# Squares in three fp32r passes: splitting the first layer's products and beginning VectorE's chain among ScalarE's first banks

## The reference

```python
B, M, D = (1024, 39, 16)
S1, S2 = (128, 128)
def _cin_layer(x0, xk, W, b):
    out = jnp.einsum('bhd,bmd,shm->bsd', xk, x0, W) + b[None, :, None]
    return jax.nn.relu(out)
e = jnp.stack([tbl_0[ids[:, 0]], ..., tbl_38[ids[:, 38]]], axis=1)
x1 = _cin_layer(e, e, W1, b1)
x2 = _cin_layer(e, x1, W2, b2)
z = jnp.concatenate([x1.sum(axis=-1), x2.sum(axis=-1)], axis=-1)
h = jnp.concatenate([z, dense_ctx], axis=1)
h = jnp.maximum(h @ W_top1 + b_top1, 0.0)
h = jnp.maximum(h @ W_top2 + b_top2, 0.0)
y = h @ W_top3
```

## Time and profile before

| | |
|---|---|
| median of three executions | 1232.25 us |
| profiled execution: time, span | 1228.31 us, 1226.4 us |
| TensorE, matmul | 1172.4 us busy, 96% |
| VectorE | 1005.4 us, 82% |
| ScalarE | 672.1 us, 55% |
| GpSimd | 864.8 us, 71% |

### The profile page before, as it was taken

The page is one execution under the profiler, slowest core; times in us unless marked ns, Lnnn a source line. Parts: engine busy times, 40 slices in busy tenths (PEclk is TensorE's granted clock), DMA queues, the critical chain, the costliest instruction groups (busy, mean ns, idle before and its releaser), DMA issues.

```text
span 1226.4 us, 17749 instructions
## 1 busy us (share of the span) xinstructions
PE 1172.4 (96%) x4784; PEld 879.4 (72%) x4784; DVE 1005.4 (82%) x3692; ACT 672.1 (55%) x2188; POOL 864.8 (71%) x836
## 2 busy tenths in 40 slices
PE   3899999999999999999999999999999999999996
PEld 2577777777777777777776667777777777777775
DVE  4298898888899888888896678888888888887695
ACT  2656666665565656556564465555655565545430
POOL 7888878888888788788776757888886454444350
PEclk9899999999999999999999999999999999999997
DMA  5000000000000000000000000000000000000000
GB/s 177 5 4 4 4 4 3 4 4 5 3 4 3 4 3 3 4 4 3 4 4 3 3 3 3 4 3 4 3 4 2 1 1 1 1 1 1 1 1 1
DMA packets 12801, 9.08 MB, mean 7 GB/s; under 512 B 6190, under 2 KB 11822, under 8 KB 12573
## 3 DMA queue, kind: packets, MB, share of 16 engines
q0 software_dynamic: 10240, 2.64, 2.6%
q1 hardware_dynamic: 2461, 5.31, 1.3%
HBM read 7.92 MB, written 0.00 MB: 6 GB/s over the span
## 4 chain that ended last, share of the span: by engine, by line
PE 72%; DVE 18%; ACT 5%; issue 2%; POOL 2%; DMA 0%; SPq 0%; ACTq 0%
PE ps L724 17%; PE ps L726 17%; PE ps L725 17%; DVE acc L634 15%; PE ps L702 13%; PE ps L690 3%; PE ps L755 3%; ACT e L464 2%; ACT fy L425 2%; POOL looked L339 2%; DVE x1l L595 1%; PE ps L678 1%; DVE e_hl L580 1%; PE ps L697 0%; DVE e_hl L583 0%
## 5 line engine op out<-in xcount | busy, mean ns | idle before, releaser
L634 DVE SCALAR_TENSOR_TENSOR acc<-ps,e,acc 128x128 f32<-128x128 f32 x3200 | 854.4, 343 | 155.7 <-PE ps L726 152.4
L724 PE MATMUL ps<-w2h,x1h 128*128 128x512 f32 (+1 forms) x1280 | 582.4, 455 | 24.9 <-ACT fy L425 13.8
L348 POOL TENSOR_TENSOR fy<-fy 128x512 f32<-128x512 f32 (+1 forms) x256 | 403.0, 1574 | 214.3 <-ACT fy L425 193.5
L425 ACT ACTIVATE fy<-ps,e 128x128 f32<-128x128 f32 x1536 | 418.1, 387 | 198.8 <-PE ps L726 198.3
L726 PE MATMUL ps<-w2h,x1l 128*128 128x512 f32 (+1 forms) x1280 | 495.4, 387 | 0.0
L725 PE MATMUL ps<-w2l,x1h 128*128 128x512 f32 (+1 forms) x1280 | 494.3, 386 | 0.0
L339 POOL DMA_INDIRECT looked<-in_table,rows x320 | 310.9, 972 | 79.1 <-issue 55.0
L724 PEld LDWEIGHTS ps<-w2h,x1h 128*128 128x128 f32 x1280 | 241.5, 189 | 134.1 <-DVE acc L634 50.9
L725 PEld LDWEIGHTS ps<-w2l,x1h 128*128 128x128 f32 x1280 | 241.6, 189 | 82.6 <-issue 44.7
L726 PEld LDWEIGHTS ps<-w2h,x1l 128*128 128x128 f32 x1280 | 240.7, 188 | 48.4
L444 ACT ACTIVATE z<-ps 128x512 f32<-128x512 f32 x192 | 117.9, 614 | 224.8 <-PE ps L690 219.5
(11 more groups left out here) (64 smaller groups left out, 385.5 us busy)
## 6 DMA issues: line engine op xcount, KB each, us to landing
looked<-in_table,rows POOLq DMA_INDIRECT x320, 2.3
w_st<-in_w SPq DMA_DIRECT2D x1, 1728.0 KB, 10.2
wt_sb<-in_wt SPq DMA_DIRECT2D x2, 512.0 KB
w_st<-in_w SPq DMA_DIRECT2D x1, 768.0 KB, 6.3
w_sb<-in_w1a SPq DMA_DIRECT2D x1, 448.0 KB, 3.2
w1b_sb<-in_w1b SPq DMA_DIRECT2D x1, 448.0 KB, 3.8
sel_st<-in_sel SPq DMA_DIRECT2D x1, 234.0 KB
ids_sb<-in_ids SPq DMA_DIRECT2D x1, 150.0 KB, 4.9
```

The costliest lines, as they stand in the source:

```text
L348: nc.gpsimd.tensor_tensor(out, a, b, ALU.add).then_inc(s_fsum, 1)
L425: nc.scalar.activation(fy[:, p % 2, sub, m - MD, :], ps[:, 2 * (nth % RING) + sub, k * S:(k + 1) * S], ACT.Copy, scale=emb(p, sub, m)).the ...
L634: nc.vector.scalar_tensor_tensor(acc[:, sub, :] if m < MD - 1 else y, y, emb(p, sub, m), acc[:, sub, :] if m else fsum[:, p % 2, sub, :], ...
L724: nc.tensor.matmul(y, x1h[:, t % 2, at], w2h[:, cols], start=True, stop=False)
```

## The change

It has three parts.

1. From tile 2 on, chunks 0, 2, 3 and 5 of the squares are split. ScalarE writes a rounded square zh, and then squares once more in place in PSUM; VectorE subtracts (zl = square - zh); TensorE takes three fp32r matmuls in place of one fp32 matmul. The next use of PSUM bank 7 waits for zl. The first layer's weights are split once at the start (w1h by ScalarE, w1l by VectorE).
2. The first banks are ordered anew: A0, D0, A1, D1, A2 of pair 0, and then the rest of pair 0 with five A banks between. In pairs 0 and 1 VectorE's chain starts with a multiplication alone, and fsum is added just before the last field. ScalarE makes the half w2h for its fields. Products of the low part of the first bank wait for x1l, the others for x1h alone.
3. TensorE runs 28 matmuls without use before the first transpose. Steps of the perceptron at slots 14 and 16 of a tile move to 8 and 14. hid1, hid2 and y_sb are laid over w2_st.

The diff, cut to its core:

```diff
+SPLIT, SPLIT_FROM = (0, 2, 3, 5), 2
+LATE = 2
+WARM = 28
 def bank_order():
-    slots = [[("A", 0, a) for a in range(A_BANKS)] + [("A", 1, a) for a in range(EARLY)]]
-    for p in range(PAIRS):
+    slots = [[("A", 0, 0), ("D", 0, 0), ("A", 0, 1), ("D", 0, 1), ("A", 0, 2)]]
+    first = (("D", 0, 2), ("D", 0, 3), ("A", 1, 0), ("D", 0, 4), ("D", 0, 5), ("A", 1, 1), ("D", 0, 6), ("A", 1, 2), ("A", 2, 0))
+    slots += [[bank] for bank in first] + [[]]
+    for p in range(1, PAIRS):
...
+def split_after(p, j):
+    slots = [s for s, kind in enumerate(ORDER) if kind == "D"] + [SLOTS]
+    return [at for s in range(slots[j], slots[j + 1]) for at in layer1_steps(p, s) if is_split(*at)]
...
-    for c, s in enumerate((0, 4, 14, 16)):
+    for c, s in enumerate((0, 4, 8, 14)):
...
-    MLP_AT[TILE_SLOTS * (tile + 1) + 14] = (g, 3, 0)
+    MLP_AT[TILE_SLOTS * (tile + 1) + 8] = (g, 3, 0)
... (ScalarE)
+                    if is_split(t, v):
+                        nc.scalar.activation(zh[:, k % 2, :], src, ACT.Square).then_inc(s_z1, 1)
+                        nc.scalar.activation(src, src, ACT.Square).then_inc(s_sq, 1)
+                    else:
+                        nc.scalar.activation(z1[:, k % 2, :], src, ACT.Square).then_inc(s_z1, 1)
...
+                nc.scalar.activation(w2h[:, MD * S:], w2_st[:, MD * S:], ACT.Copy, scale=0.5).then_inc(s_w2h, 1)
+                nc.scalar.activation(w1h[:], w1_sb[:, 0:C1, :], ACT.Copy).then_inc(s_w1h, 1)
... (VectorE)
+                def square_low(t, v):
+                    k = C1 * t + v
+                    dve.wait_ge(s_sq, splits(t, v))
+                    if k >= 2:
+                        dve.wait_ge(s_mm1, k - 1)
+                    nc.vector.tensor_tensor(zl[:, k % 2, :], ps[:, BK_T, :], zh[:, k % 2, :], ALU.subtract).then_inc(s_zl, 1)
...
+                            if m == MD - 1 and p < LATE:
+                                dve.wait_ge(s_fsum, ADDS_PER_PAIR * (p + 1))
+                                dve.wait_ge(s_stt, n)
+                                for sub in range(2):
+                                    nc.vector.tensor_tensor(acc[:, sub, :], acc[:, sub, :], fsum[:, p % 2, sub, :],
+                                                            ALU.add).then_inc(s_late, 1)
...
+                        for at in split_after(p, j):
+                            square_low(*at)
... (TensorE)
-                            pe.wait_ge(s_z1, C1 * at[0] + at[1] + 1)
+                            if is_split(*at):
+                                pe.wait_ge(s_zl, splits(*at))
+                            else:
+                                pe.wait_ge(s_z1, C1 * at[0] + at[1] + 1)
...
+                    if is_split(t, v):
+                        nc.tensor.matmul(ps[:, BK_ACC1, :], w1h[:, v, :], zh[:, k % 2, :], start=False, stop=False)
+                        nc.tensor.matmul(ps[:, BK_ACC1, :], w1l[:, v, :], zh[:, k % 2, :], start=False, stop=False)
+                        pe.wait_ge(s_zl, splits(t, v))
+                        mm = nc.tensor.matmul(ps[:, BK_ACC1, :], w1h[:, v, :], zl[:, k % 2, :], start=False, stop=(v == C1 - 1))
...
+                for _ in range(WARM):
+                    nc.tensor.matmul(ps[:, C1 - 1, :], sel_r[:, 0, :], sel_r[:, 0:N // K1, :].rearrange("p c k -> p (c k)"),
+                                     start=True, stop=True)
```

More of the change, by code:

```diff
@@ L120, in layer1_steps, with is_split, splits @@
     return [(t, k // 2)] if t < TILES and k % 2 == 0 and k // 2 <= C1 and slot >= 11 else []
+def is_split(t, v):
+    return t >= SPLIT_FROM and v in SPLIT
+def splits(t, v):
+    return sum(is_split(u, w) for u in range(t + 1) for w in range(C1) if (u, w) <= (t, v))
+def split_after(p, j):
+    slots = [s for s, kind in enumerate(ORDER) if kind == "D"] + [SLOTS]
+    return [at for s in range(slots[j], slots[j + 1]) for at in layer1_steps(p, s) if is_split(*at)]
 def put_by_dve(f):
@@ L209, in cin_tower @@
         wz = sb("wz", [P, S], F32R)
+        w1h = sb("w1h", [K1, C1, S], F32R)
+        w1l = sb("w1l", [K1, C1, S], F32R)
         fold_sb = sb("fold_sb", [K1, C1, M])
@@ L215, in cin_tower @@
         z1 = sb("z1", [P, 2, N])
+        zh = sb("zh", [P, 2, N], F32R)
+        zl = sb("zl", [P, 2, N], F32R)
         x1 = sb("x1", [S, 2, N])
@@ L265, in cin_tower @@
         s_wz = sem("s_wz")
+        s_w1h = sem("s_w1h")
+        s_w1l = sem("s_w1l")
         s_z1 = sem("s_z1")
+        s_sq = sem("s_sq")
+        s_zl = sem("s_zl")
+        s_late = sem("s_late")
         s_mm1 = sem("s_mm1")
@@ L328, in _ @@
                 sp.wait_ge(s_tail, 7)
-                sp.dma_start(out, y_sb[:]).then_inc(s_out, 16)
+                sp.dma_start(out, y_sb).then_inc(s_out, 16)
                 sp.wait_ge(s_out, 16)
@@ L513, in _ @@
                 high_part(1)
[L514 to L517, removed]
+                for n, (kind, p, j) in enumerate(BANK_SLOTS[0]):
+                    if kind == "A":
+                        scaled_fields(p, j)
+                    if n == 0:
+                        products_high(1)
+                    if n == 3:
                         turned(1)
@@ L613, in _ @@
                 low_part(0)
-                dve.wait_ge(s_w2a, 16)
-                split_w2(slice(MD * S, M * S))
+                dve.wait_ge(s_w2h, 1)
+                w2_low(slice(MD * S, M * S))
                 dve.wait_ge(s_w2d, 16)
-                split_w2(slice(0, MD * S))
+                nc.vector.tensor_scalar(w2h[:, 0:MD * S], w2_st[:, 0:MD * S], 0.5, None, ALU.mult).then_inc(s_w2h, 1)
+                dve.wait_ge(s_w2h, 2)
+                w2_low(slice(0, MD * S))
+                dve.wait_ge(s_w1h, 1)
+                nc.vector.tensor_tensor(w1l[:], w1_sb[:, 0:C1, :], w1h[:], ALU.subtract).then_inc(s_w1l, 1)
                 first_layer_low(0)
@@ L633, in _ @@
                                 y = ps[:, 2 * (nth % RING) + sub, k * S:(k + 1) * S]
+                                if m == 0 and p < LATE:
+                                    nc.vector.tensor_scalar(acc[:, sub, :], y, emb(p, sub, m), None, ALU.mult).then_inc(s_stt, 1)
+                                    n += 1
+                                    continue
                                 nc.vector.scalar_tensor_tensor(
```

43 lines of the change are left out of this document (26 added, 17 removed).

## The result

| | before | after |
|---|---|---|
| median (us) | 1232.4 | 1261.1 (1259.54 to 1263.33) |
| ratio | | 1.0234 [1.0216, 1.0251] |
| profiled execution, span | 1228.31, 1226.4 | 1260.78, 1258.9 |

The forecast was 1250, range 1224 to 1257. The direction came out, and so did the waits for zl that were to make the tiles slower; the sum did not: the time lies 4 us above the range. A second measurement on another chip gave 1254.92 beside 1226.96, ratio 1.0225 [1.0208, 1.0242]. The traced execution of before is 4.1 us shorter than its median, that of the changed kernel is at it, so the spans lie 32.5 us apart where the medians lie 28.7 apart.

What follows compares the result with a forecast made beforehand. TensorE (96% busy) was taken as bound, with stretches where VectorE sets the end. Steady state -21.6+5.4+17.5+11.1+4.7 = +17.1 us, start +1.3, on the profiled 1228.3: 1246.7; median 3.9 higher, 1250.6, called 1250, range 1224 to 1257.

Steps and rivals of the forecast that it cites:

- The gain on TensorE: Split products on TensorE: three passes take 0.68 us in place of 0.86, 120 times, 21.6 us less.
- Chunk 5 gains nothing: Chunk 5's product, behind D2 of the even pair: TensorE waits afterwards for what it saves, 5.4 us of the gain go.
- The wait for zl of chunk 0: Odd pair: chunk 1's expansion comes 4.88 us after J, D0's start on VectorE, at the earliest; 17.5 us lost together.
- The wait for zl of chunk 3: Behind D5: chunk 4's expansion waits until 4.88 us after D4's start, 0.37 us 30 times, 11.1 us lost.
- The zl of chunks 2 and 5: They lie in VectorE's idle time and cost nothing; without that cover each would cost up to 0.7 us.
- Steady state: Sum over the tiles of passes, chunk 5, both zl waits and restarts: +17.1 us.
- restart: First TensorE matmul after each wait takes 0.33 us instead of 0.23; booked as 59 x 0.08 = 4.7 us.
- The start: Up to chunk 1's expansion in tile 0's odd pair: 77.7 us against 76.37 before, +1.3 us.
- w1l and w2h: Weight splits at the start: new w1l on VectorE, w2h's smaller part leaving it, about balancing in cost to look-ups.
- the waits don't bind: Rival: VectorE's zl arrives in time and TensorE keeps its pace; about 1212 us, or 1207; chance 0.14.
- Slower by ScalarE: Rival: two squares delay ScalarE's scalings 0.5 us, fsum comes later, VectorE's D0 waits; 1250, up to 1260 us; chance 0.09.
- VectorE's share: Sign in the profile after: VectorE is busy 87 to 88% of the time.

Runs made afterwards that it cites:

- e7: e5 with chunk 5 unsplit, its product fp32 again: 1213.60 us, ratio 0.9892 to before.
- e9: The changed kernel measured again without any edit, on another chip: 1254.92 us, ratio 1.0225 to before.
- e3: The changed kernel's split alone, on the start of before (old bank order, no late sums, no warm-up matmuls): 1253.21 us, ratio 1.0172 to before.
- e12: The kernel before, unchanged, profiled once more: 1225.83 us in its one execution.
- e10: e4 without the 28 warm-up matmuls: 1221.46 us, ratio 0.9958 to before.
- e11: e5 with the late sums of the changed kernel added, old bank order kept: 1215.73 us, ratio 0.9912 to before.
- e1: The changed kernel with no chunk split, so its new start alone: 1239.86 us, ratio 1.0061 to before.
- e2: e1 without the 28 warm-up matmuls: 1237.72 us, ratio 1.0038 to before.
- e4: The changed kernel with zl of chunks 0 and 3 after the first four instructions of D1 and D5: 1230.11 us, ratio 0.9979 to before.
- e5: e4 with the start of before (old bank order, no late sums, no warm-up matmuls): 1213.84 us, ratio 0.9887 to before.
- e8: The changed kernel with tile 2's ten look-ups issued behind the sums of pair 0 on GpSimd: 1267.37 us, ratio 1.0328 to before.

## Why the prediction was wrong, step by step

- *The gain on TensorE*: right. The three passes take 0.70 at 597.45 (0.68 forecast).
- *Chunk 5 gains nothing*: right (e7).
- *The wait for zl of chunk 0*: right, J + 4.86 measured for 4.88, and 4.86 to 4.98 in every tile from 1 to 29, fill or not; zl is 682 ns for 0.68. TensorE's load queue waits for zl 56 times in the changed kernel's first trace and 59 times in e9; 59 were counted.
- *The wait for zl of chunk 3*: right, 4.88. The zl of chunks 2 and 5 cost nothing, as booked: behind that of chunk 2 VectorE still waits 0.43 us for D4 (603.57).
- *Steady state*, +17.1: the mechanism was right, the size 3 us too small. Counted from the expansion of chunk 1 in tile 0 to the end of the span, it is 18.5 in e3, 19.3 in the changed kernel's first trace (89.56 and 76.37, 1258.9 and 1226.4) and 20.5 in e9 against e12 (83.73 and 74.72, 1253.5 and 1224.0). A restart costs 0.11 us (597.11 to 597.45 against 0.23); the sum booked 0.08, though its own row gives 0.10. What is missing lies in two tiles. From D0 of the odd pair of tile 21 to that of tile 22 it is 38.89 in e9 (855.35 to 894.24) and 36.61 in e12 (832.62 to 869.23), 2.28 more, and from tile 25 to 26 2.22 more; the recorded terms give 0.2 each. All other tiles together come out some 0.7 us below theirs. In both places the even pair holds a four-tile fill. Its low part now runs beside GpSimd's additions: the last difference takes 1.48 us in e9 and 0.40 in e12, and D6 then waits 0.98 us for TensorE, in e12 0.35.

```profile
889.70 1.48 DVE L629 TENSOR_TENSOR e_hl<-prod,e_hl 128x240 f32<-128x240 f32 x1
892.16 1.13 DVE L700 SCALAR_TENSOR_TENSOR acc<-ps,e,acc 128x128 f32<-128x128 f32 x4 [0.98 <-PE ps L809]
866.40 0.40 DVE L583 TENSOR_TENSOR e_hl<-prod,e_hl 128x240 f32<-128x240 f32 x1
```

- *The start*, +1.3: this is the step that failed. It was a walk over durations to "71.2 for the pair's end, 72.85 for D0, 77.7 for the expansion of chunk 1". In e9 these are 75.25, 78.28 and 83.73, and before on such a chip (e12) D0 was at 71.03 and the expansion at 74.72: +9.0 us. Three things make up the 5.4 us between 72.85 and 78.28:
  1. The 28 warm-up matmuls, 2.6 us (e9 against e10). They took 632 ns each, 12.3 us in all, so the transposes that feed the first layer started at 24.57, in e12 at 20.47. I had bounded this by 1 us.
  2. The late sums take 2.10 for 0.6. The operation was sized rightly, but not its neighbour: the first of the two takes 0.28 us and the second 1.90 (e9, from 72.20), until 0.16 us behind the end of an addition of GpSimd. In e11, without such an addition beside them, the two together take 0.51.
  3. The bank behind p takes 3.02 for 1.65. TensorE had waited 5.71 us for p, and its matmuls then come every 0.43 us; in 74 to 78 us its granted clock is 0.50, the 1.2 GHz level (below). I had walked at 2.4 GHz.

  With 2.6, 1.5 and 1.4 that is 5.5, the whole of it. Of the other 2.3 us, 1.6 are before's: its D0 is at 72.67 in the trace that was read and at 71.03 in e12. The rest is the first odd pair's own: the expansion comes at J + 5.45, with D1 waiting 0.27 us for TensorE. The mechanism that I named (the low part waits for ScalarE's high part, all else stands behind it) is there, 1.57 us at 76.52 in the changed kernel. Two stretches of e9 (us from and to, length, busy us and count of TensorE, its loads, VectorE, ScalarE and GpSimd, then the granted clock):

```profile
12.00:24.00 12.00, 12.00 (x30) 9.22 (x29) 6.21 (x14) 5.13 (x15) 9.56 (x9) 1.00 0.59 195
74.00:78.00 4.00, 2.69 (x6) 2.07 (x7) 1.19 (x5) 0.00 (x0) 3.25 (x5) 0.50 0.01 2
```

- *Two standstills* in the changed kernel's first trace, until 25.6 and 48.9 us:

```profile
25.61 0.60 ACT L468 ACTIVATE x0t<-ps 128x512 fp32r<-128x512 f32 x1 [5.11 <-remote]
48.89 1.40 ACT L461 ACTIVATE fy<-ps,e 128x128 f32<-128x128 f32 x5 [6.90 <-remote]
```

  The first stands in the place of the warm-up's price: there the 28 matmuls took only 7.3 us and the transposes started at 20.79, but ScalarE's copy of their result came at 25.61 all the same, in e9 at 25.66, in before at 22.16. So the 2.6 us of item 1 are e9's; in the trace of the result the same delay has another source. The second, of ScalarE and VectorE, is in the changed kernel, e1, e2, e3 and e4, ending between 48.6 and 49.0 whatever they were at; e5 to e12, on three other chips, don't have it, and before's trace doesn't either. With it D0 of the first odd pair is 5.9 us later in the changed kernel (84.18, e9 78.28) and 4.8 in the old order (e3 76.25, e5 71.45). It hardly shows in the result: the medians lie 28.7 us apart there and 28.0 beside e9, since before too took 5 us longer there (1232.4 and 1227.0). That its untraced executions had the standstill is likely, but not shown, and the cause stays open.
- *w1l and w2h*: nothing, as booked (w1l is 0.95 us in VectorE's idle time).

The range missed by 4 us. The start, whose gain I bounded at 14.8 us, got no loss beyond 1.3, although it was the longest chain of assumed durations in the sum. Its 9.0 us and the 20.5 of the tiles make the 29.5 by which the spans of e9 and e12 differ.

Of the rivals, "the waits don't bind" (20 us gained) describes another kernel than this one: once zl stands where it hardly binds, 13.9 us are gained (e5). It had forgotten the 5.4 us of chunk 5, which go in any case (e7). "Slower by ScalarE" had VectorE's D0 wait for fsum; in the changed kernel's trace and in e9 VectorE never waits for it. VectorE's share came to 86% for 87 to 88, since the span grew.

## What to carry to other kernels

Ask of every added instruction in front of whom it is queued: the same 120 instructions cost 20 us when all stood at the end of a bank (e3), and the kernel gained 14 us when 60 of them stood four instructions into it (e5). An engine's long wait at the start is worth nothing until the next engine's order is walked through as well. The idle stretch of 5.7 us that the new order gave TensorE had a bank at half clock behind it, and that belongs in the sum. And a VectorE operation with two SBUF inputs is priced by what GpSimd does beside it.

## What was not expected of the hardware

- VectorE's operations with two SBUF inputs took up to nearly seven times their shortest length, and the wait stands inside the row, not as idle time. The long ones of 128 and 156 columns end 0.16 to 0.19 us behind the end of an addition of GpSimd: the second late sum of e9 at 74.10 for 73.94 (first row below), the low part in before's trace at 70.54 for 70.35 (the other two rows); so does L626 of the changed kernel, 2.01 us from 72.93 (0.32 in e10 at 37.71, beside look-ups). The first late sum of e9 takes 0.28 beside a look-up. The Trainium skill, "SBUF — State Buffer", section "SBUF: two separate sides", has a VectorE operation with two SBUF inputs and a GpSimd operation that reads SBUF take turns at one port pair, where the one that starts second is fully blocked. The long rows agree. In one of them the order of the starts doesn't: the second late sum starts at 72.20, the addition at 72.67.

```profile
72.67 1.27 POOL L382 TENSOR_TENSOR fy<-fy 128x512 f32<-128x512 f32 x1
69.07 1.28 POOL L348 TENSOR_TENSOR fy<-fy 128x512 f32<-128x512 f32 x1 [0.52 <-POOL fy L348]
69.39 1.15 DVE L580 TENSOR_TENSOR e_hl<-e,e_hl 128x156 f32<-128x156 f32 x1
```

- The same 28 warm-up matmuls took 7.0 us in e8 and 7.3 in e4 and in the changed kernel's first trace, and 12.3 in e1 and e9, where they come every 0.43 us, the spacing of the half clock above. What decides between the two was not tried. In this early stretch of e9 the granted clock reads 1.00 all the same, so there the matmuls' own durations (ns, first and last start) are the ones to read:

```profile
L849 PE MATMUL ps<-sel_r x28: 632/632/796, 12.5 to 24.1; 78*128 78x512 f32 x28
```
